# A new order of the end, and of the first batch's V projections, in an attention and expert kernel

## The reference, cut to what matters

```
x = x + attention(cond(x, f, f, w, u, t), W_K, W_Q, W_V, W_O)
y2 = cond2(x, f, f, w2, u2, t)
logits = y2 @ gate_w.T                    # 8 experts
top_w, top_i = top_k(logits, 2); gates = softmax(top_w) at top_i, else 0
x = x + sum_e gates[:, e] * (y2 @ expert_w[e] + expert_b[e])
```

## Time and profile before

| | us |
|---|---|
| median of 3 runs | 381.71 (381.62 to 381.79) |
| the profiled execution's own time | 381.94 |
| its span | 380.1 |
| TensorE busy | 351.5 (92%) |
| VectorE busy | 317.6 (84%) |
| ScalarE busy | 255.8 (67%) |
| GpSimd busy | 212.3 (56%) |

### The profile page before, as it was taken

How to read it: one execution, slowest core, us unless ns; L and a number is a source line. 1 busy time by engine, 2 the same in 40 slices (tenths; PEclk the granted TensorE clock), 3 DMA queues, 4 the chain that set the end, 5 groups by cost and what they waited for, 6 DMA issues and landing times.

```text
span 380.1 us, 7412 instructions
## 1 busy us (share of the span) xinstructions
PE 351.5 (92%) x2404; PEld 323.6 (85%) x2404; DVE 317.6 (84%) x883; ACT 255.8 (67%) x685; POOL 212.3 (56%) x223
## 2 busy tenths in 40 slices
PE   0897789999999999999999999999999998798997
PEld 0686679999999999899999999999999886685785
DVE  4979899999898988999899989998676747476576
ACT  5678888788778878877987889787877643210100
POOL 1865677864647669767857966886744341210000
PEclk9998899999999999999999999999999999898999
DMA  5660130100000000130100041000000000000000
GB/s 170 243 252 3 55 112 0 58 3 0 2 0 3 2 0 2 55 114 2 55 2 1 3 166 57 3 1 2 0 3 2 1 0 2 0 29 1 28 29 28
DMA packets 4597, 14.12 MB, mean 37 GB/s; under 512 B 840, under 2 KB 1872, under 8 KB 3920
## 3 DMA queue, kind: packets, MB, share of 16 engines
q1 hardware_dynamic: 4336, 13.65, 10.6%
q10 hardware_dynamic: 224, 0.01, 0.0%
HBM read 12.60 MB, written 1.05 MB: 36 GB/s over the span
## 4 chain that ended last, share of the span: by engine, by line
PE 67%; DVE 25%; issue 4%; ACT 3%; DMA 1%; DVEq 0%; ACTq 0%
PE psQK L900 7%; PE psQK L902 7%; PE psQK L901 7%; PE psT L970 4%; PE psO L900 4%; DVE tiles L703 3%; PE psO L902 3%; PE psO L901 3%; PE psS L900 3%; PE psS L901 3%; PE psS L902 3%; PE psV L900 3%; PE psS L956 3%; PE psZ L983 3%; PE psV L902 3%
## 5 line engine op out<-in xcount | busy, mean ns | idle before, releaser
L313 POOL TENSOR_SCALAR prob<-prob,rsum 128x256 f32<-128x256 f32 x60 | 55.7, 928 | 62.2 <-DVE rsum L738 62.2
L900 PE MATMUL psQK<-y_hi,w_hi 128*128 128x256 f32 x256 | 73.1, 286 | 1.2 <-DVE y_lo L653 1.2
L902 PE MATMUL psQK<-y_hi,w_lo 128*128 128x256 f32 x256 | 73.0, 285 | 0.0
L901 PE MATMUL psQK<-y_lo,w_hi 128*128 128x256 f32 x256 | 73.0, 285 | 0.0
L496 ACT ACTIVATE prob<-prob,ntop 128x256 f32<-128x256 f32 (+1 forms) x128 | 57.2, 449 | 23.3 <-DVE ntop L730 23.1
L319 POOL TENSOR_TENSOR z_lo<-z_lo,z_two 128x256 fp32r<-128x256 f32 x64 | 47.9, 748 | 36.0 <-DVE z_lo L756 36.0
L278 POOL TENSOR_TENSOR w_lo<-raw,w_hi 128x512 fp32r<-128x512 f32 x40 | 53.6, 1352 | 12.1 <-ACT w_hi L372 12.1
L900 PEld LDWEIGHTS psQK<-y_hi,w_hi 128*128 128x128 f32 x256 | 49.4, 193 | 3.1 <-issue 1.6
L901 PEld LDWEIGHTS psQK<-y_lo,w_hi 128*128 128x128 f32 x256 | 49.5, 194 | 1.3
L902 PEld LDWEIGHTS psQK<-y_hi,w_lo 128*128 128x128 f32 x256 | 49.5, 194 | 0.0
L742 DVE TENSOR_TENSOR qk<-psQK,qk 128x512 fp32r<-128x512 f32 x64 | 43.2, 676 | 6.0 <-ACT qk L484 6.0
(11 more groups left out here) (159 smaller groups left out, 1041.8 us busy)
## 6 DMA issues: line engine op xcount, KB each, us to landing
raw<-in_weights SPq DMA_DIRECT2D x5, 1024.0 KB, 5.2
raw<-in_weights SPq DMA_DIRECT2D x10, 512.0 KB, 4.2
out<-fT SPq DMA_DIRECT2D x8, 128.0 KB, 1.7
fT<-in_fT SPq DMA_DIRECT2D x2, 256.0 KB, 5.0
xT<-in_xT SPq DMA_DIRECT2D x2, 256.0 KB, 6.7
fT<-in_fT SPq DMA_DIRECT2D x1, 512.0 KB, 6.1
xT<-in_xT SPq DMA_DIRECT2D x1, 512.0 KB, 6.0
temb<-in_temb ACTq DMA_DIRECT2D x1, 1.0 KB, 3.4
```

Source lines behind the costliest of these rows:

```text
L313: pool.tensor_scalar(prob[:, k, P:3 * P], prob[:, k, P:3 * P], rsum[:, k, 1:2], None, ALU.mult).then_inc(shared, 1)
L900: pe.matmul(out, ah, bh, start=first and k == 0, stop=False)
L901: pe.matmul(out, ah, bl, start=False, stop=False)
L902: ins = pe.matmul(out, al, bh, start=False, stop=last and k == n - 1)
```

## The change

In block 0 alone (i == 0), the V projection of units 1 and 2 moves behind `project_qk(u + 2)` on TensorE, `v_high` behind `qk_high(u + 2)` on ScalarE, and `v_low` behind `qk_low(u + 2)` on VectorE. At the end the same pieces are done in another order on the three engines. No instruction is added or removed.

```diff
--- before.py
+++ after.py
@@ -559,31 +559,33 @@
             if u >= 2:
                 pT_high(u - 2)
             exps(u)
-            if 1 <= h <= TT:
+            if 1 <= h <= TT and i > 0:
                 v_high(i, h - 1)
             do(u, "M")
             if u + 2 < UNITS:
                 qk_high(u + 2)
+            if 1 <= h <= TT and i == 0:
+                v_high(i, h - 1)
             if u >= 3:
                 z_high(u - 3)
             shares(u)
             do(u, "E")
+        pT_high(UNITS - 2)
         z_high(UNITS - 3)
-        pT_high(UNITS - 2)
         gate_exp(1)
+        pT_high(UNITS - 1)
         tanh(2)
         z_high(UNITS - 2)
-        pT_high(UNITS - 1)
         z_high(UNITS - 1)
         y2_high(2)
         gates_copy(1)
         tanh(3)
         base_copy(1)
+        y2_high(3)
         gate_exp(2)
-        y2_high(3)
         gates_copy(2)
+        gate_exp(3)
         base_copy(2)
-        gate_exp(3)
         gates_copy(3)
         base_copy(3)
 
@@ -858,38 +860,42 @@
             do(u, "M")
             reciprocals(u)
             i, h = u // GH, u % GH
-            if 1 <= h <= TT:
+            if 1 <= h <= TT and i > 0:
                 v_low(i, h - 1)
             if u + 2 < UNITS:
                 qk_low(u + 2)
+            if 1 <= h <= TT and i == 0:
+                v_low(i, h - 1)
             if u >= 3:
                 z_low(u - 3)
             do(u, "E")
+
+        pT_low(UNITS - 2)
         z_low(UNITS - 3)
-        pT_low(UNITS - 2)
         gate_first(1)
         add_experts(1)
         add_output(14)
+        add_experts(2)
+        pT_low(UNITS - 1)
+        gate_last(1)
         z_low(UNITS - 2)
-        pT_low(UNITS - 1)
-        add_experts(2)
-        gate_last(1)
         y2_last(2)
+        add_experts(3)
         z_low(UNITS - 1)
-        add_experts(3)
-        add_experts(4)
+        for j in range(4, 7):
+            add_experts(j)
         add_output(15)
-        add_experts(5)
+        y2_last(3)
         gate_first(2)
-        add_experts(6)
-        y2_last(3)
-        gate_last(2)
         add_experts(7)
         add_experts(8)
+        gate_last(2)
+        add_experts(9)
+        add_experts(10)
         gate_first(3)
-        add_experts(9)
+        add_experts(11)
         gate_last(3)
-        for j in range(10, 8 * B):
+        for j in range(12, 8 * B):
             add_experts(j)
 
     @block.tensor
@@ -1087,10 +1093,13 @@
             scores(u)
             if u == UNITS - 2:
                 experts(0)
-            if 1 <= h <= TT:
+
+            if 1 <= h <= TT and i > 0:
                 project_v(i, h - 1)
             if u + 2 < UNITS:
                 project_qk(u + 2)
+            if 1 <= h <= TT and i == 0:
+                project_v(i, h - 1)
             if u >= 3:
                 values(u - 3)
             if h == 3 and i >= 1:
@@ -1104,22 +1113,22 @@
             if u == UNITS - 3:
                 gates_turn(0)
             if u >= UNITS - 2:
+                if u == UNITS - 1:
+                    values(UNITS - 3)
                 experts(u - UNITS + 3)
-        values(UNITS - 3)
+        output(len(BLOCKS) - 2, 1)
+        turn(UNITS - 1)
         experts(3)
-        turn(UNITS - 1)
-        output(len(BLOCKS) - 2, 1)
         values(UNITS - 2)
         experts(4)
         values(UNITS - 1)
         experts(5)
+        gates_turn(1)
+        experts(6)
         for c in range(CB):
             output(len(BLOCKS) - 1, c)
-        gates_turn(1)
         base(1)
-        experts(6)
-        logits(2)
-        late = {8: [(logits, 3)], 10: [(gates_turn, 2)], 12: [(base, 2)], 14: [(gates_turn, 3)], 16: [(base, 3)]}
+        late = {7: [(logits, 2)], 10: [(logits, 3)], 11: [(gates_turn, 2)], 13: [(base, 2)], 15: [(gates_turn, 3)], 17: [(base, 3)]}
         for j in range(7, 8 * B - 1):
             experts(j)
             for f, b in late.get(j, ()):
```

## The result

The changed kernel takes 371.86 us (median of 4, 371.76 to 371.87) against 381.75 us (381.62 to 381.81) of the kernel before beside it: a ratio of 0.9741, 95% interval 0.9724 to 0.9758. The forecast was 371.6. Its profiled execution has a span of 370.0 us against 380.1. Run again with the last series of experiments, the changed kernel took 371.68 us (371.62 to 371.78) and the kernel before 379.92 (378.5 to 382.87), ratio 0.9772 (0.9733 to 0.9810): the changed kernel is the same in both, and the kernel before scatters. Why that is so came out of the experiments.

The account below looks back on a forecast made before the run. TensorE was taken as the bound between 53 and 300 us. The end's 9.4 and the front's 0.7 make 10.1: 381.94 - 10.1 = 371.8, less 0.2 for the median, 371.6 us; range 370.4 to 375.0.

Parts of the forecast that it names:

- What bounds the kernel, the dense stretch: TensorE is the bound between 53 and 300 us, at clock 1.00, with no idle entry from 53.24 to 300.44.
- The front, 0.7: Block 0: `project_qk(4)` runs in TensorE's 2.83 us wait, VectorE's reciprocal starts earlier, gaining 0.7 us; bounds -0.6 to 0.9.
- a late V costs nothing: Front: V(0,1) starts near 32.35 instead of 31.75 us, yet ends before `turn(1)` can begin, at no cost.
- the last front wait would come 0.7 us earlier: Sign of being right: TensorE's last front wait, 1.25 us up to 53.24, begins and ends 0.7 us earlier.
- TensorE's own work at the end, 36.3: From 311.71 us to the start of `experts(18)`, 31 pieces sum to 36.3 us, where the kernel before takes 46.4.
- The one wait, 0.6: End: `values(63)` waits 0.6 us on TensorE for `z_low(62)`, which follows `gate_last(1)` on VectorE.
- The other waits: End: TensorE's waits of 2.06 and 1.84 us, one half-microsecond wait and that of `base(1)` go; smallest later margin 1.8 us.
- The clock: End: half-clock stretches of 3.4 and 3.7 us behind waits of 2.06 and 1.84 go with them; none behind 0.92.
- (a): Rival: the end is repaired, the front gives nothing or loses 0.6 us: 372.3 to 372.9 us; chance 0.13.
- (b): Rival: a new end wait, at `values(63)` or VectorE's backlog, brings a low-clock stretch: 3.0 more, 374.6 us; chance 0.13.
- (c): Rival: only half the end's idle time goes, VectorE coming late more than once: 376 to 377 us; chance 0.07.
- (d): Rival: slower, the clock staying low over the end; 385.6 us if for 30 us; chance 0.03.

Follow-up runs that it names:

- the end alone: The changed kernel with the front's three swaps taken out again: 372.46 us.
- the short fill: The kernel before plus 16 unread split-operand matmuls, eight inside each of TensorE's waits of 2.06 and 1.84 us: 378.65 us, ratio 0.9949.
- e6: The changed kernel without ScalarE's and VectorE's front swaps, and on VectorE `z_low(62)` ahead of `gate_last(1)`, `z_low(63)` right behind it: 370.72 us.
- e8: The changed kernel with the old places and VectorE's and ScalarE's old order behind `base(1)`: 374.61 us, in groups 373.75 to 373.88 and 375.35 to 375.69.
- ScalarE's one swap: The changed kernel with `gate_exp(3)` put back behind `base_copy(2)` on ScalarE: 372.24 us.

## Why the prediction was right

- **What bounds the kernel, the dense stretch.** Right. TensorE is at a clock of 1.00 from 52.6 us on, and what the front gained arrived at the end undiminished. One reading was wrong: between 53.24 and 300.44 us there are idle entries, 0.78 us at 158.98 and 0.24 at 194.37. Both kernels have them, so the forecast didn't feel it.
- **The front, 0.7.** The mechanism was right and the size was off: 0.99. The reciprocal moved by 0.76 (37.63 to 36.87) as worked out, and up to `v_low(1,0)` VectorE's chain gained 0.25 more, 0.2 of it by a clamp that took 0.36 instead of 0.56 us. It took 0.56 in the three profiles in which VectorE had waited for Q and K just before (the kernel before, the end alone, the short fill), and 0.35 or 0.36 in the ten others; why is open. What the step missed is that the wait it removes depends on the clock: 0.66, 0.27 or 0 us in three profiles of the old order. So 0.99 is the gain over an execution with the fall; over one without it there is none. The statement that a late V costs nothing held: V(0,1) began at 32.38 (32.35 forecast), `turn(1)` at 34.90. The sign that the last front wait would come 0.7 us earlier could not show: the wait isn't in this profile.
- **TensorE's own work at the end, 36.3.** 37.13 less the wait's 1.06 is 36.07.
- **The one wait, 0.6.** It came where it was said, at `values(63)` behind `gate_last(1)`, and was 1.06 from start to start (0.88 as idle time). `gate_first(1)` took 1.35 instead of 1.06, its gap alone 0.45 instead of 0.16, beside GpSimd's `z_last` at 312.73. The total didn't show it, because four errors cancel: the front gave 0.3 more than forecast and TensorE's own work took 0.2 less, while the wait cost almost 0.5 more and the tail 0.1 more. That the total came within 0.3 us is partly luck.
- **The other waits.** All gone, as followed through. VectorE restarted at 329.57, `gates_turn(2)` found the gates 1.7 us old where the smallest margin was to be 1.8.
- **The clock.** That waits of 2.06 and 1.84 us let it fall and 0.9 does not was right as to the cause, which the filled waits show, but the working took both falls as fixed. They are not: they come in some executions and not in others. Where both come, the gain is 9.9 us. All executions measured with the result stood at 381.6 to 381.9, which fits that, though only one has a profile. In the last series the gain is between 6.8 (against 378.5) and 10.0 (against 381.7), or 11.2 against the one at 382.87, and by the medians 8.2. The forecast of 371.6 us holds in both series; the forecast gain of 10.1 holds only against executions with both falls.
- **The rivals.** None of (a) to (d) happened. That (b)'s place was the weak one is shown by e6, which takes 1.0 us more from it, and e8 shows what a returned wait costs, 2.1 us without the fall and, if its slower group is the fall, 3.8 with it; (b) had 3.0 for one grown by 1.2.

## What to carry to other kernels

Where one engine is gapless for most of the span, work out the ends piece by piece from start to start, and then follow every in-order queue through the new order; the sum of the pieces gives the ceiling, and the waits that you find are what is left below it. A wait of about 2 us on TensorE costs itself and sometimes the low clock behind it, so it is worth more than its length and it scatters the times: if a kernel's times stand in groups, look for such waits, and judge by the groups, not by the medians. Before a piece is moved ahead into a wait, look for what it needs itself: here the swap that pays in block 0 gains nothing in block 1, where V's matmuls had covered GpSimd's refill, and loses where the clock is low.

## What the runs showed of the hardware that was not expected

A plain float32 matmul of 256 columns took 0.41 us from start to start at a clock of 1.00 (eight of them, on record as 16 rows, 3.26 us), a split one 0.12 to 0.14 (eight, 1.11 us). And the granted clock fell behind the same wait in one execution and not in the next: behind 2.83 us at 31.7 it was 0.53 in one profile and 1.00 in another, behind 2.04 to 2.06 us 0.50 and 1.00, behind 2.00 to 2.01 us at 32.3 0.55 (the changed kernel) and 1.00 (the late half as before), behind 1.84 0.54 and 1.00. In the thirteen profiles, from 30 us on, every stretch at about half clock stands behind a wait of 1.84 to 2.83 us, and none behind a wait of 1.70 us or less. Such a stretch cost nothing where another engine set the pace: the changed kernel has one at 45.5 us (0.61), the kernel with ScalarE's one swap has none there, and from first scores to `turn(62)` they take 288.15 and 288.07 us.
